# Last layer as seven block products: 2048x1024 rows times a 1024x1024 four-bit weight, on one core

## The chip, the cores and the metric

The kernel runs on 1 core of one Trainium2 chip. The metric is device time in microseconds (us) of one execution; the median of several executions counts. Times of single instructions come from one profiled execution.

## The reference

Two layers, each added to its input. The change is in the second one; the first is shown by its end only.

```python
x = x + xattn(layernorm(x), ctx, ctx, pos, mask, Wq, Wk, Wv, Wo)      # ends in 2048x4096 @ 4096x1024
x = x + ffn(layernorm(x), qweight, qzeros, scales, bias)

def ffn(x, qweight, qzeros, scales, bias):                           # x: 2048 x 1024
    w = (qweight[:, None, :] >> shifts & 15).reshape(1024, 1024)     # 4-bit numbers out of int32 words
    W = repeat(scales, 128) * (w - repeat(zeros, 128))
    return x @ W + bias
```

All is float32. The kernel makes each float32 product of a high and a low part per operand (hi*hi + hi*lo + lo*hi), so one 128x128 by 128x512 block costs three matmuls.

## The kernel before

The end of the kernel has two stages. The **output projection** (attention times Wo, added onto the rows of x) is already done as seven block products instead of eight, in the order M1, M7, M4, M5, M3, M2, M6. Each has 16 steps (PAIRS), so there are 112 steps (STEPS), numbered s = 0 to 111. One step is `block_step`: 8 blocks of rows, each into its own bank of `ps` (PSUM), three matmuls of 512 columns each (lines 823 to 825), 24 matmuls in all. The row tiles 0 to 7 are called EVEN, 8 to 15 ODD; their sums grow in `rows`.

Every engine walks the same steps in an order written out by hand, and each step passes through all of them. SP loads the left operand into `xring` (`load_left`) and the right one into `wraw` (`load_right`), two buffers each, and waits ahead of each for the low part two steps back. ACT (`step_hi`, lines 1045 and 1050) waits until TensorE has finished step s - 2, and writes the high parts into `a_parts` and `b_parts`, two slots each. VectorE (`step_lo`, line 1365) subtracts for the left low part, GpSimd (`step_lo`, line 1664) for the right one; in M1, M7, M4, M3 and M6 GpSimd first adds two right blocks (`right_summed`, line 1676). TensorE waits for both low parts. After each product VectorE adds the eight banks onto `rows` (`product_out`, line 1483), in the step with s % 16 == 1; products that go to two places are first copied by ACT into `spare` (line 1129) and added again later (line 1490). M6's eight banks end in ODD rows, right half, after the last step.

Beside these steps the kernel before prepares the **last layer**: VectorE and ACT unpack W into `w_parts` (high and low part, `DENSE_AT`, lines 1495 to 1504), and the statistics of the layer norm of the EVEN rows are taken in steps 82 to 92 (`row_stats`, `inverse_std`). The last layer then goes row tile by row tile, r = 0 to 15: VectorE normalizes (`y_normalize`, line 1510, which reads every eighth word of a row), TensorE transposes eight 128x128 blocks (`y_fill`, line 847), ACT and VectorE split the result into high and low part, and TensorE multiplies with all of W: `dense(r)`, 2 halves x 8 blocks of k x 3 matmuls (`products`, lines 244 to 246). VectorE adds the result onto the row tile (line 1569), to which GpSimd has added the bias (line 1720), and SP stores it. Statistics of the ODD rows are taken during the first row tiles.

In the program, waits are semaphores: `eng.wait_ge(name, n)` stops that engine's whole queue until n is reached, and `.then_inc(name, n)` counts up when the instruction is done.

Of the kernel before, what the change touches and what calls it, by code (L numbers as in the profile page):

```python
# [15 lines left out]
P = 128  # L16
# [36 lines left out]
V_H0_N0, K_H0, V_H0_N1, V_H1_N1, K_H1, V_H1_N0 = 0, 8, 24, 32, 40, 56  # L53

# [14 lines left out]
def build(nc, x, ctx_t, x_tiles, x_pieces, pos, mask, wq, wk, wv, wo, qweight, qzeros, scales, bias, table, ident, out):  # L69
# [4 lines left out]
    with ExitStack() as stack:  # L74
# [44 lines left out]
        with ExitStack() as late:  # L119
# [5 lines left out]
            dense = sb_c("dense", [P, 4, E], F32)  # L125
            rows = sb_c("rows", [P, 16, E], F32)
            w_parts = sb_c("w_parts", [P, KT, 2, E], F32R)
            zero_words = sb_c("zero_words", [P, E // NIB], I32)
            bias_rows = sb_c("bias_rows", [P, E], F32)
            spare = sb_c("spare", [P, 8, NW], F32)  # L130

# [6 lines left out]
        sq_dram = dram("sq_scratch", [4, P, 4, S])  # L138

# [39 lines left out]
        packed, scale_rows = dense[:, 0, :].bitcast(I32), dense[:, 1, :]  # L179
        zeros_f, w_full = dense[:, 2, :].bitcast(I32), dense[:, 3, :]  # L180
        xn = [dense[:, i, :] for i in range(4)]
        x2t = [a_parts[:, i, :, :].rearrange("p l (k t) -> p l k t", k=KT) for i in range(2)]
# [47 lines left out]
        z_step, dq_step, wf_full, wf_hi, wf_lo = sem("z_step"), sem("dq_step"), sem("wf_full"), sem("wf_hi"), sem("wf_lo")  # L230
        y_norm, y_done, y_hi, y_lo = sem("y_norm"), sem("y_done"), sem("y_hi"), sem("y_lo")
# [4 lines left out]
        ffn_done, ffn_added, biased = sem("ffn_done"), sem("ffn_added"), sem("biased")  # L236
# [57 lines left out]
        DENSE_AT = (25, 28, 34, 37, 40, 43, 54, 57)  # L294


        @block.sync
        def _(sp):
# [281 lines left out]
            for s in range(4, STEPS):  # L580
# [17 lines left out]
                if s == 22:  # L598
                    sp.dma_start(zero_words[:, :],
# [5 lines left out]
            for r in range(16):  # L605
                if r < 15:
                    sp.wait_ge(ffn_added, 2 * r + 2)
                    sp.dma_start(o_rows[row_tile(r)], rows[:, r, :]).then_inc(out_stored, 16)
                else:
                    for n in range(2):  # L610
                        sp.wait_ge(ffn_added, 2 * r + n + 1)
                        sp.dma_start(o_rows[row_tile(r)][:, n * NW:(n + 1) * NW], rows[:, r, n * NW:(n + 1) * NW]
                                     ).then_inc(out_stored, 16)
            sp.wait_ge(out_stored, 17 * 16)
# [3 lines left out]
        def _(pe):  # L618
# [218 lines left out]

            def y_fill(f):
                r = f // 2
                pe.wait_ge(y_norm, r + 1)  # L840
                if f < 2:
                    pe.wait_ge(m_out, 48 + f + 1)
                else:
# [912 lines left out]
```

## Time and profile before

| | us |
|---|---|
| median of 3 runs | 2243.64 (2242.38 to 2246.56) |
| the profiled execution | 2245.39 |
| span of its first to last instruction | 2243.6 |
| TensorE busy | 2225.5 (99%) |
| VectorE, ACT, GpSimd busy | 1370.2, 1052.7, 1394.0 |
| output projection ends, last layer begins | at 2050.6 of the span |
| mean granted clock of TensorE | 0.998 of full speed |

The page of the profile gives busy time per engine and the costliest groups of instructions. Beside it the trace answers questions: instructions in order of time, groups by line, the chain of waits that ended last, and busy time, clock and DMA rate in chosen stretches. A matmul's printed duration is longer than the distance to the next one, since matmuls are pipelined: what a step costs is read from the distance of its repeats.

### The profile page before, as it was taken

Reading aid. Unit: us, or ns where it says so; the run is one execution under the profiler, and the core shown is the slowest. Engines: PE = TensorE matmul, PEld = TensorE weight load, DVE = VectorE, ACT = ScalarE, POOL = GpSimd, SP = SyncE. Lnnn points to the kernel's source line nnn. Section 1 sums busy time; section 2 is a strip of 40 time slices with the busy share of each in tenths; the row PEclk is TensorE's granted clock in tenths of the full one; section 3 lists DMA queues with packets and bytes.
Section 4 is the critical chain, followed back from the end, with each engine's and each line's share of the span. In section 5 each row is a group of like instructions: output and inputs, shape, how many; then the busy total and the mean of one; then the engine's idle time right before and its main releaser. Section 6 shows DMA issues by size and latency. Waiting matters only on the chain.

```text
span 2243.6 us, 33219 instructions
## 1 busy us (share of the span) xinstructions
PE 2225.5 (99%) x10582; PEld 1868.4 (83%) x10582; DVE 1370.2 (61%) x2537; ACT 1052.7 (47%) x2298; POOL 1394.0 (62%) x982
## 2 busy tenths in 40 slices
PE   9999999999999999999999999899999999999999
PEld 7888888888888888788888888788888888888887
DVE  4772575777777778877777777423675445453532
ACT  3222133766766667666666766522333323331100
POOL 2320553788888889888888888665663354454210
PEclk9999999999999999999999999999999999999999
DMA  7766675687888789888888888697554554452111
GB/s 269 257 234 221 238 268 193 211 252 241 243 261 238 242 247 276 251 260 243 242 243 252 244 239 253 189 321 263 198 186 152 163 195 151 159 192 69 47 47 47
DMA packets 300187, 476.71 MB, mean 212 GB/s; under 512 B 23600, under 2 KB 195920, under 8 KB 300112
## 3 DMA queue, kind: packets, MB, share of 16 engines
q1 hardware_dynamic: 285744, 439.60, 62.4%
q10 hardware_dynamic: 13600, 34.08, 3.9%
q0 software_dynamic: 768, 2.10, 0.2%
q8 instruction: 39, 0.64, 0.1%
q14 instruction: 36, 0.29, 0.0%
HBM read 303.70 MB, written 171.98 MB: 212 GB/s over the span
## 4 chain that ended last, share of the span: by engine, by line
PE 91%; DVE 3%; POOL 3%; DMA 1%; ACT 1%; issue 1%; SPq 0%; DVEq 0%; ACTq 0%; POOLq 0%
PE ps L244 22%; PE ps L245 22%; PE ps L246 21%; PE ps L823 9%; PE ps L825 8%; PE ps L824 8%; PE ps L847 1%; POOL rope_tmp L1587 1%; DMA left_scratch<-s_buf 0%; POOL s_buf L1587 0%; DVE rope_tmp L1188 0%; DVE rope_tmp L1189 0%; DVE rope_tmp L1187 0%; ACT wq_t L891 0%; DMA wraw<-in_L_xattn_Wo 0%
## 5 line engine op out<-in xcount | busy, mean ns | idle before, releaser
L244 PE MATMUL ps<-act_t,wq_t 128*128 128x512 f32 x1280 | 500.2, 391 | 1.2 <-DVE act_t L1250 0.6
L245 PE MATMUL ps<-act_t,wq_t 128*128 128x512 f32 x1280 | 499.5, 390 | 0.0
L246 PE MATMUL ps<-act_t,wq_t 128*128 128x512 f32 x1280 | 498.0, 389 | 0.0
L1664 POOL TENSOR_TENSOR b_parts<-wraw,b_parts 128x512 fp32r<-128x512 f32 x112 | 200.3, 1788 | 267.0 <-ACT b_parts L1050 267.0
L823 PE MATMUL ps<-b_parts,a_parts 128*128 128x512 f32 x896 | 349.2, 390 | 0.6 <-DVE a_parts L1365 0.3
L824 PE MATMUL ps<-b_parts,a_parts 128*128 128x512 f32 x896 | 348.8, 389 | 0.0
L825 PE MATMUL ps<-b_parts,a_parts 128*128 128x512 f32 x896 | 348.6, 389 | 0.0
L1365 DVE TENSOR_TENSOR a_parts<-xring,a_parts 128x1024 fp32r<-128x1024 f32 x112 | 146.6, 1309 | 304.8 <-ACT a_parts L1045 304.8
L1646 POOL TENSOR_TENSOR q_t<-pt_raw,q_t 128x1024 fp32r<-128x1024 f32 x124 | 302.4, 2439 | 43.8 <-ACT q_t L1028 40.8
L1587 POOL TENSOR_TENSOR rope_tmp<-rope_tmp 128x512 f32<-128x512 f32 x144 | 193.3, 1342 | 182.7 <-DVE rope_tmp L1189 182.7
L1045 ACT ACTIVATE a_parts<-xring 128x1024 fp32r<-128x1024 f32 x112 | 118.7, 1060 | 393.3 <-PE ps L825 393.3
L246 PEld LDWEIGHTS ps<-act_t,wq_t 128*128 128x128 f32 x1280 | 240.4, 188 | 50.9
L244 PEld LDWEIGHTS ps<-act_t,wq_t 128*128 128x128 f32 x1280 | 240.8, 188 | 49.8 <-DVE act_t L1250 1.8
L245 PEld LDWEIGHTS ps<-act_t,wq_t 128*128 128x128 f32 x1280 | 240.8, 188 | 44.9
L1010 ACT ACTIVATE probs<-scores,neg_max 128x256 f32<-128x256 f32 x512 | 254.1, 497 | 3.6 <-DVE neg_max L1354 3.5
L1187 DVE TENSOR_TENSOR rope_tmp<-ps,rope 128x512 f32<-128x512 f32 x144 | 99.4, 690 | 218.7 <-PE ps L246 211.7
L1002 ACT ACTIVATE q_t<-rope_tmp 128x512 fp32r<-128x512 f32 x128 | 81.1, 634 | 321.8 <-POOL rope_tmp L1587 321.8
L1020 ACT ACTIVATE probs<-probs,inv_sum 128x256 f32<-128x256 f32 x512 | 216.8, 494 | 3.0 <-DVE inv_sum L1361 3.0
L1640 POOL TENSOR_TENSOR q_t<-rope_tmp,q_t 128x512 fp32r<-128x512 f32 x128 | 196.7, 1537 | 5.2 <-ACT q_t L1002 5.2
L823 PEld LDWEIGHTS ps<-b_parts,a_parts 128*128 128x128 f32 x896 | 168.4, 188 | 36.4 <-issue 0.9
L824 PEld LDWEIGHTS ps<-b_parts,a_parts 128*128 128x128 f32 x896 | 168.4, 188 | 35.0
L825 PEld LDWEIGHTS ps<-b_parts,a_parts 128*128 128x128 f32 x896 | 168.4, 188 | 34.8
(143 smaller groups left out, 4379.4 us busy)
## 6 DMA issues: line engine op xcount, KB each, us to landing
sq_scratch<-scores SPq DMA_DIRECT2D x124, 512.0 KB, 3.0
pt_raw<-sq_scratch SPq DMA_DIRECT2D x496, 128.0 KB, 4.0
xring<-left_scratch SPq DMA_DIRECT2D x112, 512.0 KB, 3.7
left_scratch<-s_buf SPq DMA_DIRECT2D x64, 640.0 KB, 5.3
wraw<-in_L_xattn_Wq SPq DMA_DIRECT2D x64, 512.0 KB, 4.6
wraw<-in_L_xattn_Wo SPq DMA_DIRECT2D x64, 512.0 KB, 4.5
v_scratch<-kv_t ACTq DMA_DIRECT2D x32, 512.0 KB, 3.4
k_scratch<-kv_t ACTq DMA_DIRECT2D x32, 512.0 KB, 5.0
```

The source lines that it names most:

```text
L244: eng.matmul(dst, lh, rh, start=(k == first), stop=False)
L245: eng.matmul(dst, lh, rl, start=False, stop=False)
L246: mm = eng.matmul(dst, ll, rh, start=False, stop=(k == last))
L823: pe.matmul(dst, lh, rh, start=(begins and not onto), stop=False, skip_group_check=True)
L824: pe.matmul(dst, lh, rl, start=False, stop=False, skip_group_check=True)
L825: mm = pe.matmul(dst, ll, rh, start=False, stop=ends, skip_group_check=True)
L1010: e = act.activation(probs[:, par, j, qt, :], score_v[:, par, j, qt * S:(qt + 1) * S], ACT.Exp, bias=neg_max[:, par, j, qt:qt + 1], scale= ...
L1020: e = act.activation(probs[:, par, j, qt, :], probs[:, par, j, qt, :], ACT.Copy, scale=inv_sum[:, par, j, qt:qt + 1])
L1587: pool.tensor_tensor(tmp[:, 0, :], tmp[:, 0, :], tmp[:, 1, :], ALU.add).then_inc(done, 1)
L1640: pool.tensor_tensor(q_parts[:, c, j, 1, :], rope_tmp[:, 0, :], q_parts[:, c, j, 0, :].bitcast(F32), ALU.subtract).then_inc(q_lo, 1)
L1646: pool.tensor_tensor(lo, pt_raw[:, u8 % 2, :], hi.bitcast(F32), ALU.subtract).then_inc(pt_lo, 1)
L1664: pool.tensor_tensor(b_parts[:, s % 2, 1, :], wraw[s % 2][:, 0:NW], b_parts[:, s % 2, 0, :].bitcast(F32), ALU.subtract).then_inc(right_lo, 1)
```

## The change

The last layer is done as seven block products too, with 4 steps of k each (KS = 4), so 28 steps, s = 112 to 139, in the order D_M1, D_M2, D_M6, D_M7, D_M4, D_M5, D_M3. A step has again 8 banks and 24 matmuls of 512 columns. The left operands are sums and differences of blocks of y (the normalized rows, transposed), the right ones of W.

- **W.** VectorE unpacks W in steps 25 to 56; GpSimd forms the four sums of its blocks (`weight_sum`, one of 128x512 in each of the steps 28 to 31, 38 to 41, 46 to 49, 57 to 60); SP stores all seven right operands to DRAM (`w_dram`, 12 transfers, 7.3 MB) in steps 33, 43, 51 and 62. In the last layer they are loaded back, 256 KB a step, into four half buffers of `wraw`.
- **First rows (EVEN).** Statistics in steps 82 to 88, normalized by ACT in steps 89 to 92 (`row_scaled`), two row tiles a step, transposed by VectorE (`turn_row`, 32x32 blocks; it reads words 8 apart and writes `turned`), stored to DRAM in 16 transfers of 256 KB (steps 93 to 100), and their first half loaded into `left_c` (steps 97 to 103). The bias is added by GpSimd (rows 0 to 5) and VectorE (6 and 7).
- **Second rows (ODD).** They are complete only after step 111. Statistics, normalization, 8 turns and 16 stores lie in steps 112 to 119; the first sum of them, which D_M6 needs at step 120, is `first_sum` on GpSimd in steps 118 to 121.
- **Low parts, sums, output.** ACT writes high parts (`dense_hi`, right operand first), VectorE the left low part (`dense_lo`) and the left sums (`dense_sum`, one 128x1024 operation ahead of each step of D_M6, D_M7, D_M5 and D_M3), GpSimd the right low part, and adds the product kept in `spare` twenty-four times (`add_second`). VectorE takes out eight banks after each product (`dense_out`), at the second step of the next one.
- The 128 transposes on TensorE, their splitting on ACT and VectorE, and the splitting of all of W are gone.

The diff, cut to what the steps of the last layer are made of:

```diff
+        SUMS_AT = (28, 38, 46, 57)
+        STATS_AT = (82, 83, 84, 85, 86, 86, 87, 87)
+        EVEN_AT = (89, 89, 90, 90, 91, 91, 92, 92)
+        BIAS_AT = (90, 91, 92, 93, 94, 95)
```

SP in the steps of the projection:

```diff
+                if s - 5 in SUMS_AT:
+                    k = SUMS_AT.index(s - 5)
+                    sp.wait_ge(w_summed, 4 * k + 4)
+                    sp.dma_start(w_dram[k, :, 0:4, :], w_sums).then_inc(w_stored, 16)
...
+                if 93 <= s < 101:
+                    sp.wait_ge(y_turned, 8)
+                    j, a0 = (s - 93) // 2, (s - 93) % 2 * 2
+                    for a in (a0, a0 + 1):
+                        store_turned(sp, 0, 2 * j, 2 * j + 2, a, turned_stored[j])
```

SP in the last layer (`dense_left_in` of a D_M6 step waits until the four stores of its k have landed, `turned_stored[k]` >= 128, and then loads `main[k]` and `left_b[:, k]`):

```diff
+            for s in range(STEPS, END):
+                d, k = dense_part(s)
+                if s + 2 < END:
+                    dense_left_in(s + 2)
+                if s + 3 < END:
+                    dense_right(s + 3)
+                if s == STEPS + KS + 1:
+                    sp.wait_ge(y_turned, 16)
+                    for j in range(2):
+                        for a in range(2):
+                            store_turned(sp, 1, 2 * j, 2 * j + 2, a, turned_stored[j])
+                elif s in (STEPS + KS + 2, STEPS + KS + 3):
+                    j = s - STEPS - KS
+                    for a in range(4):
+                        store_turned(sp, 1, 2 * j, 2 * j + 2, a, turned_stored[j])
...
```

TensorE:

```diff
+            def dense_step(s):
+                d, k = dense_part(s)
+                pe.wait_ge(left_lo, s + 1)
+                pe.wait_ge(right_lo, s + 1)
...
+                        elif d == D_M2:
+                            pe.wait_ge(d_copied, i + 1)
+                        else:
+                            pe.wait_ge(d_out, 8 * (d - 2) + i + 1)
...
```

ACT in the last layer:

```diff
+            for s in range(STEPS, END):
+                dense_hi(s)
+                if s == STEPS + 1:
+                    root(3, 8, 4)
+                    act.wait_ge(y_turned, 8)
+                if s == STEPS + 2:
+                    for r in range(8, 11):
+                        row_scaled(xn[:, r % 4, :], r)
+                    root(4, 12, 4)
...
+                if s == STEPS + KS + 1:
+                    act.wait_ge(y_turned, 16)
+                    for j in range(2):
+                        for a in range(2, 4):
+                            store_turned(act, 1, 2 * j, 2 * j + 2, a, turned_stored[j])
+                if s == STEPS + KS:
+                    act.wait_ge(m_added, 32)
+                    for i in range(8):
+                        bank_ready(act, D_M1, i)
+                        act.activation(spare[:, i, :], ps[:, i, :], ACT.Copy).then_inc(d_copied, 1)
```

VectorE (`dense_sum` of a D_M6 step waits for `s1_made` >= k + 1; what is left out at STEPS + 2 does for rows 12 to 15 what stands above for rows 8 to 11):

```diff
+            def turn_row(src, r):
+                dve.transpose(turned_v[:, r % 8], src.rearrange("p (b i k) -> p k b i", b=4, k=KT)).then_inc(y_turned, 1)
...
+            for s in range(STEPS, END):
+                d, k = dense_part(s)
+                if k == 1:
+                    if d > D_M2:
+                        dense_out(d - 1)
+                dense_lo(s)
+                if s + 1 < END:
+                    dense_sum(s + 1)
+                if s == STEPS:
+                    product_out(M6)
+                    for r in range(8, 12):
+                        dve.wait_ge(m_out, 48 + r - 8 + 1)
+                        half_stats(r, 1)
+                elif s == STEPS + 1:
+                    inverse_std(2, 8, 4)
+                    mean_scaled(8, 4)
+                elif s == STEPS + 2:
...
+                if STEPS + 2 <= s < STEPS + 5:
+                    for r in ((8,), (9, 10, 11), (12, 13, 14, 15))[s - STEPS - 2]:
+                        dve.wait_ge(y_act, r + 1)
+                        turn_row(xn[:, r % 4, :] if r < 12 else left_b[:, r % 4, :], r)
+                elif s in (STEPS + 6, STEPS + 7):
+                    for r in (2 * (s - STEPS), 2 * (s - STEPS) + 1):
+                        row_biased(r)
```

GpSimd:

```diff
+            def first_sum(k):
+                pool.wait_ge(main_in[k], 2 * 16)
+                pool.wait_ge(side_in[k], 32)
+                pool.tensor_tensor(left_b[:, k, :], left_b[:, k, :], main[k], ALU.add).then_inc(s1_made, 1)
...
+            for s in range(STEPS, END):
+                d, k = dense_part(s)
+                step_lo(s)
+                if STEPS + 2 <= s < STEPS + 6:
+                    pool.wait_ge(y_act, 8 + s - STEPS - 1)
+                    add_bias(8 + s - STEPS - 2)
+                elif STEPS + 6 <= s < STEPS + 10:
+                    first_sum(s - STEPS - 6)
+                elif d == D_M7:
...
+                    for i in (2 * k, 2 * k + 1):
+                        add_second(i, rows[:, ODD + i, NW:E])
```

## Rows read from the trace of the kernel before

**Rows 1.** The page: busy time of each engine (part 1) and mean DMA rate (part 3).
```profile
PE 2225.5 (99%) x10582; PEld 1868.4 (83%) x10582; DVE 1370.2 (61%) x2537; ACT 1052.7 (47%) x2298; POOL 1394.0 (62%) x982
...
HBM read 303.70 MB, written 171.98 MB: 212 GB/s over the span
```
**Rows 2.** The chain that ended last: start us, us, engine, tile, line.
```profile
2050.61 0.45 PE ps L847 x4
...
2076.45 0.87 PE ps L847 x8
...
2240.15 0.24 PE ps L246
2240.42 0.69 DVE rows L1569
```
**Rows 3.** Timeline of VectorE, end of the projection: start us, us, [idle before].
```profile
2035.42 1.23 DVE L1365 TENSOR_TENSOR a_parts<-xring,a_parts 128x1024 fp32r<-128x1024 f32 x1 [4.21 <-ACT a_parts L1045]
2040.86 1.23 DVE L1365 TENSOR_TENSOR a_parts<-xring,a_parts 128x1024 fp32r<-128x1024 f32 x1 [4.21 <-ACT a_parts L1045]
2045.88 5.46 DVE L1483 TENSOR_TENSOR rows<-ps,rows 128x512 f32<-128x512 f32 x8 [3.80 <-PE ps L825]
...
2068.17 3.64 DVE L1213 BATCH_NORM_STATS2 stats<-rows 128x6 f32<-128x512 f32 x6
```
**Rows 4.** Timeline of ACT and GpSimd, same steps.
```profile
2039.76 1.06 ACT L1045 ACTIVATE a_parts<-xring 128x1024 fp32r<-128x1024 f32 x1 [3.86 <-PE ps L825]
2040.73 0.62 ACT L1050 ACTIVATE b_parts<-wraw 128x512 fp32r<-128x512 f32 x1
...
2037.75 1.29 POOL L1676 TENSOR_TENSOR wraw<-wraw 128x512 f32<-128x512 f32 x1
2041.42 1.81 POOL L1664 TENSOR_TENSOR b_parts<-wraw,b_parts 128x512 fp32r<-128x512 f32 x1 [2.38 <-ACT b_parts L1050]
2043.19 9.45 POOL L1720 TENSOR_TENSOR rows<-rows,bias_rows 128x1024 f32<-128x1024 f32 x4
```
**Rows 5.** Timeline of VectorE at step 92: the layer norm of eight row tiles.
```profile
1937.90 0.71 DVE L1221 BATCH_NORM_AGGREGATE mean_var<-stats 128x2 f32<-128x12 f32 x8
...
1940.29 0.17 DVE L1235 TENSOR_TENSOR inv_std<-ln_tmp 128x8 f32<-128x8 f32 x1
```
**Rows 6.** VectorE by line and form, whole span: its transposition.
```profile
L1371 DVE STREAM_TRANSPOSE scores<-probs 128x1024 f32<-128x1024 f32 x124 | 154.4, 1245 | 4.2 <-ACT probs L1020 0.3
```
**Rows 7.** Timeline: VectorE beside GpSimd, two pairs, and VectorE alone.
```profile
1589.17 1.81 POOL L1664 TENSOR_TENSOR b_parts<-wraw,b_parts 128x512 fp32r<-128x512 f32 x1 [2.01 <-ACT b_parts L1050]
1589.75 1.78 DVE L1495 TENSOR_SCALAR dense<-dense 128x1024 int32<-128x1024 int32 x1
...
1948.21 1.81 POOL L1664 TENSOR_TENSOR b_parts<-wraw,b_parts 128x512 fp32r<-128x512 f32 x1 [3.56 <-ACT b_parts L1050]
1948.79 2.25 DVE L1510 TENSOR_SCALAR dense<-rows,mean_var,inv_std 128x1024 f32<-128x1024 f32 x1
...
2066.99 1.26 DVE L1510 TENSOR_SCALAR dense<-rows,mean_var,inv_std 128x1024 f32<-128x1024 f32 x1
```
**Rows 8.** DMA by issue: tiles, count, KB each, median us to landing.
```profile
xring<-left_scratch SPq DMA_DIRECT2D x112, 512.0 KB, 3.7
wraw<-in_L_xattn_Wo SPq DMA_DIRECT2D x64, 512.0 KB, 4.5
...
out<-rows SPq DMA_DIRECT2D x2, 256.0 KB, 2.0
```
**Rows 9.** Stretches: busy us of each engine, granted clock, DMA share, GB/s.
```profile
1426.00:1428.00 2.00, 2.00 (x18) 1.86 (x17) 0.78 (x2) 0.62 (x2) 0.04 (x1) 1.00 1.01 344
...
1432.00:1434.00 2.00, 0.00 (x0) 0.00 (x0) 2.00 (x5) 1.84 (x6) 2.00 (x3) 1.00 0.00 0
1434.00:1436.00 2.00, 1.44 (x6) 1.20 (x7) 0.41 (x1) 0.98 (x3) 0.51 (x1) 0.89 0.23 81
1436.00:1438.00 2.00, 2.00 (x11) 1.80 (x9) 0.69 (x1) 0.00 (x0) 0.00 (x0) 0.50 1.02 242
```

More of the change, by code:

```diff
@@ L53 @@
 V_H0_N0, K_H0, V_H0_N1, V_H1_N1, K_H1, V_H1_N0 = 0, 8, 24, 32, 40, 56
+D_M1, D_M2, D_M6, D_M7, D_M4, D_M5, D_M3 = range(7)
+D_RIGHT = (4, 5, 1, 2, 3, 0, 6)
+KS = KT // 2
 TILES = ((0, 0), (1, 0), (0, 1), (1, 1))
@@ L604, in _ @@
                                  ).then_inc(bias_in, 16)
[L605 to L613, printed above, removed]
@@ L617, in _ @@
+            for i in range(8):
+                sp.wait_ge(d_out, 32 + i + 1)
+                store_half(8 + i, 1)
+            for i in range(8):
+                sp.wait_ge(d_out, 40 + i + 1)
+                store_half(i, 1)
+            sp.wait_ge(out_stored, 32 * 16)
         @block.tensor
@@ L1129, in product_copied, with root, row_scaled @@
                     act.activation(spare[:, i, :], ps[:, i, :], ACT.Copy).then_inc(m_spared, 1)
+            def root(value, first, n):
+                act.wait_ge(ln_var, value)
+                act.activation(ln_tmp[:, 1, first:first + n], ln_tmp[:, 0, first:first + n], ACT.Sqrt).then_inc(ln_root, 1)
+            def row_scaled(dst, r):
+                act.wait_ge(ln_less, max(r // 4, 1))
+                act.activation(dst, rows[:, r, :], ACT.Identity, bias=ln_tmp[:, 3, r:r + 1],
+                               scale=inv_std[:, r:r + 1]).then_inc(y_act, 1)
             for s in range(2, STEPS):
@@ L1153, in _ @@
-            for f in range(32):
-                dense_fill_hi(f)
-                if f == 11:
-                    act.wait_ge(ln_var, 3)
-                    act.activation(ln_tmp[:, 1, 8:16], ln_tmp[:, 0, 8:16], ACT.Sqrt).then_inc(ln_root, 1)
+                if s == 88:
+                    root(2, 0, 8)
+                if s in EVEN_AT:
+                    for r in range(8):
+                        if EVEN_AT[r] == s:
+                            if r >= 4:
+                                act.wait_ge(y_turned, r - 3)
+                            row_scaled(xn[:, r % 4, :], r)
@@ new lines, in dense_out @@
+            def dense_out(d):
+                for i in range(8):
+                    bank_ready(dve, d, i)
+                    if d == D_M6:
+                        dve.wait_ge(d_copied, i + 1)
+                        dst = spare[:, i, :]
+                    elif d == D_M2:
+                        if i < 6:
+                            dve.wait_ge(biased, i + 1)
+                        else:
+                            dve.wait_ge(biased_v, i - 5)
+                        dst = rows[:, EVEN + i, 0:NW]
+                    elif d == D_M3:
+                        dve.wait_ge(u_added, 16 + i + 1)
+                        dst = rows[:, EVEN + i, NW:E]
+                    elif d == D_M4:
+                        dve.wait_ge(u_added, 8 + i + 1)
+                        dst = rows[:, ODD + i, 0:NW]
+                    else:
+                        dve.wait_ge(u_added, i + 1)
+                        dst = rows[:, ODD + i, NW:E]
+                    dve.tensor_tensor(dst, ps[:, i, :], dst, ALU.add).then_inc(d_out, 1)
@@ L1577, in _ @@
+            dense_out(D_M3)
         @block.gpsimd
```

347 lines of the change are left out of this document (230 added, 117 removed).

## The prediction

> **What bounds the kernel now.** First the busy times: TensorE is busy for 99% of the span [rows 1], so the time is TensorE's work plus its waits. Then the chain that ended last: from 2050.61 to 2240.39 (2240.15 + 0.24) it is TensorE, with 0.87 us of transpositions in each row tile, and behind it one addition of 0.69 and a store [rows 2]. So the last layer is 189.8 us of TensorE and a tail of 3.2. Third, the timelines of one step of the projection: VectorE's low part returns after 2040.86 - 2035.42 = 5.44 us [rows 3], which is the price of 24 matmuls, 0.227 each. In every step VectorE waits 4.21 ahead of its low part, ACT 3.86, GpSimd 2.38 [rows 3, 4]: that is the cover for new work. The last step begins at 2050.61 - 5.44 = 2045.17; VectorE has its low part at 2042.09 and GpSimd at 2043.23, so they may be 3.1 and 1.9 late before TensorE waits.
>
> **The change part by part.** Below, 0 is the end of step 111 (2050.61); numbers are us.
>
> TensorE. 28 steps of 5.44 are 152.3 instead of 189.8: **-37.5**, if nothing is late. The tail stays: the last product's banks end 0.68 apart, VectorE adds each in 0.69 [rows 2, 3], and a store of 256 KB takes 2.0 [rows 8], as now.
>
> W. A sum on GpSimd takes 1.29 (the row of the same shape) and falls into its gap of 2.38 [rows 4]; sixteen of them would be 20.6 without that gap. Each of the four store groups is 1.84 MB, 5.3 at 344 GB/s [rows 9], in SP's queue ahead of loads that are issued two steps early and now land after 3.7 to 4.5 [rows 8]. Without that cover steps 33 and 43, which load 512 KB of right operand, lose some 2 each, so 0 to 4; I take 0.
>
> One turn. VectorE's transposition of 128x1024 takes 1.245 [rows 6], but that one reads 32 words side by side. The new one reads words 8 apart, as line 1510 does now. How much that costs is in [rows 7]: in both pairs VectorE begins while GpSimd is at work, waits, and goes on when GpSimd ends. Line 1495 (1024 words side by side) ends 1591.53 - 1590.98 = 0.55 after GpSimd; line 1510 (1024 words, 8 apart) 1951.04 - 1950.02 = 1.02 after it: 1.85 times. So a turn lies between 1.25 (line 1510 is slow for another reason) and 1.245 x 1.85 = 2.3; it handles as many words as the old one, which excludes less. I take **2.3**, since line 1510 reads these very rows in this very pattern. The Trainium skill (Advanced Engine Details and Errata, Memory Cachelines) says that SBUF is read in lines of 16 bytes and that a pattern which goes to another line with each access pays a penalty; words 8 apart are 32 bytes apart. By that rule the sum is the one of the forecast below, without it that of the first rival; [rows 7] agree with it, no row shows a transposition that reads so.
>
> First rows, steps 89 to 103. Two turns and a low part are 5.8 per step, more than 5.44, and VectorE's subtraction waits for GpSimd's bias addition of 2.37 (9.45 / 4) [rows 4] which begins in the meantime: in steps 91, 92 and 93 the low part comes about 6.5 after the step before has begun, three waits of 1.05. The eighth turn ends 4.5 after the start of step 92. SP waits for it with the loads of step 94 queued behind, and two stores go ahead of these; they are issued some 3.5 late and land behind 512 KB, which costs 1.9 more. Together **+5.0**; with turns of 1.25 (3.7 per step) nothing. DMA at steps 96 to 103 is 1.6 to 2.1 MB a step, 4.6 to 6.1 at 344 GB/s, inside the two steps that loads run ahead.
>
> Second rows, the head of the layer. VectorE's queue after step 111 decides. It holds: low part of 112, M6's eight additions (5.5, to 3.3), four half statistics (0.61 each, to 5.7), low part of 113 (to 6.95). Step 113 was due at 5.44: wait 1.6. Then the layer norm of four tiles (for eight it took 2.6, 1937.90 to 1940.46 [rows 5]), in which ACT stands at the root with the high parts of 114 queued behind; low part of 114 at 11.0, in time. Four more statistics and the second layer norm, to 15.8; turn of row 8, to 18.1; low part of 115 behind a bias addition on GpSimd, 19.8, due 17.95: wait 2.0. Three turns, low part of 116 at 27.9, due 25.35: wait 2.6. Four turns, to 37.1, low part of 117 at 38.3, due 33.45: wait 5.0. Sum **+11.2**. With turns of 1.25 the last turn ends at 29.65 and the waits are 1.6, 2.0, 0 and 0.75: +4.4.
>
> The way through DRAM. At 37.1 SP and ACT, both waiting for the last turn (ACT with the high parts of 118 behind it, still in time), issue eight stores of 256 KB, 2.1 MB, 6.1 at 344 GB/s. SP then waits for the first half, with the right operands of 121 and later queued behind, and issues loads of 1.05 MB, which queue behind the second half: they land at about 50. GpSimd's first sum (2.4, to 52.4) has the right low part of step 119 queued behind it: step 119 starts at 53.8, due 49.3: wait 4.5. Each further k moves 1.05 MB of stores, 1.05 of loads and 0.26 of right operand, 6.9; the second sum ends at 59.3, then VectorE's left sum, and behind that the eight additions of D_M2, of which TensorE needs the first for step 120: wait about 4. Step 121 loses about 1, step 122 none. Sum **+9.5**. These 9.2 MB need 27 at 344 GB/s and 38 at 242, the lowest rate of a full stretch [rows 9]: 0 to 11 more.
>
> D_M7 to D_M3. In steps 125, 133 and 137 VectorE has 5.5 of additions, a low part and a sum (1.23 each): 8.0 against 5.44 and a reserve of 3.1, less what GpSimd holds it up (up to 1.29): 0.1 to 1.4 each, **+2.5** with the fourth. In six steps GpSimd's three operations (3.9) and VectorE's two (2.2) exclude each other, 6.1 of 5.44: if all of that shows, 9 instead of 2.5.
>
> The clock. Between 1432 and 1434 TensorE did nothing; right after, the granted clock fell from 1.00 to 0.89 and 0.50 in the next stretches [rows 9], half of 2.4 GHz. Two such us lose one. The waits ahead of steps 115 to 121 are as long, but most slowed steps end before the next operand is there. I take **+1.5**, 0 to 5.
>
> Sum: -37.5 + 5.0 + 11.2 + 9.5 + 2.5 + 1.5 = **-7.8**. The profiled execution would go from 2245.39 to 2237.6 (span 2243.6 to 2235.8); the median of the runs shown lies 1.75 lower than that execution, so I predict 2243.64 - 7.8 = 2236.
>
> **The rivals.**
> - Cheap turns (1.25): -37.5 + 0 + 4.4 + 9 + 2.5 + 1.5 = -20: **2223.5**. For it: the only row of a transposition [rows 6]. Against: [rows 7].
> - Cheap turns, and the stores and loads land before they are missed: -37.5 + 4.4 + 2.5 = -30.6: **2213**. Against it: two transfers in a row, 2.0 and 3.7 at the least [rows 8], under 4 MB of others.
> - The DMA is slower, and the time ends **above before**: strips of 32 partitions in pieces of 1 KB move at the mean rate of the span, 212 GB/s [rows 1], so the 9.2 MB ahead of step 122 need 43 instead of 27: +16, **2252**, all of it in waits ahead of 119 to 122. It decides from 233 GB/s down (+12.3, 2248.1). For it: 242 in a full stretch. Against: 344 in another [rows 9].
> - VectorE and GpSimd hold each other up in D_M7 to D_M5: +6.5, **2242.5**, no change that shows. For it: 6.1 of 5.44. Against: the operations of both have reserves of a few us.
>
> **How the numbers follow.** A measurement of this kernel can tell about 0.2%, 4.5 us, from no change: faster is below 2239.1, slower above 2248.1. Chances: forecast 0.46 (own range 2229 to 2243: 0.36 faster, 0.08 same, 0.02 slower), cheap turns 0.27, all hidden 0.05, slow DMA 0.14 (0.12 slower, 0.02 same), mutual holding 0.08 (0.06 same, 0.02 faster). Together faster 0.70, same 0.16, slower 0.14. The range goes from cheap turns with a third less waiting (2216) to the DMA bound of 242 GB/s on the forecast and a little more (2249); it leaves out all hidden and most of slow DMA, 0.17.
>
> **What would show it.** The transposition's row in the last layer: 2.3 or 1.25. TensorE idle ahead of steps 91 to 94, with VectorE's low part as what ended it. In the last layer, idle of TensorE ahead of 113, 115, 116 and 117 ended by VectorE's low part, ahead of 119 by GpSimd's, and GpSimd's first sum waiting for a DMA. From step 122 on 5.44 a step. TensorE's work is wrong if a step takes longer than 5.44 without a wait. The prediction is wrong if waits stand in steps 28 to 62, if the loads of the ODD rows land much later than 13 after the last turn, or if the last product's stores end later than 3.2 after the last matmul.

## The result and the profile after

| | before | after |
|---|---|---|
| median of the runs side by side, us | 2245.10 | 2234.15 (2231.84 to 2235.26) |
| ratio, 95% interval | | 0.995 (0.9938 to 0.9962) |
| the profiled execution, us | 2245.39 | 2235.26 |
| its span, us | 2243.6 | 2233.5 |
| step 112 starts (last layer begins) | 2050.61 | 2052.52 |
| last matmul ends | 2240.39 | 2230.1 |
| last layer on TensorE | 189.8 | 177.6 |

The forecast was 2236, faster. The interval of the ratio lies below 1: the kernel is 0.4 to 0.6% faster. In the page of the changed kernel (busy time per engine), which answers [rows 1], TensorE is busy for 28.6 us less:

```profile
PE 2196.9 (98%) x10358; PEld 1838.8 (82%) x10358; DVE 1436.9 (64%) x2575; ACT 1094.6 (49%) x2339; POOL 1493.0 (67%) x1048
```

The last layer is 12.2 us shorter. Its 28 steps are 152.3 without waits, so 25.3 are lost in it; the forecast had 24.7 there (11.2 + 9.5 + 2.5 + 1.5). TensorE's own timeline shows where it stands (start us, us, in brackets the idle time before and what ended it):

```profile
2058.72 0.50 PE L976 MATMUL ps<-b_parts,a_parts 128*128 128x512 f32 x1 [0.60 <-DVE a_parts L1718]
...
2074.26 0.79 PE L976 MATMUL ps<-b_parts,a_parts 128*128 128x512 f32 x1 [4.36 <-DVE a_parts L1718]
2074.85 0.63 PE L977 MATMUL ps<-b_parts,a_parts 128*128 128x512 f32 x1
2075.28 0.63 PE L978 MATMUL ps<-b_parts,a_parts 128*128 128x512 f32 x1
...
2090.55 0.68 PE L976 MATMUL ps<-b_parts,a_parts 128*128 128x512 f32 x1 [2.24 <-DVE a_parts L1718]
...
2106.17 0.47 PE L976 MATMUL ps<-b_parts,a_parts 128*128 128x512 f32 x1 [2.85 <-POOL b_parts L1881]
...
2115.66 0.77 PE L976 MATMUL ps<-b_parts,a_parts 128*128 128x512 f32 x1 [3.77 <-DVE rows L1757]
```

These are the starts of steps 113, 115, 117, 119 and 120. The next matmul follows 0.43 after the one before (2074.85, 2075.28) instead of 0.227: behind this wait of 4.36 TensorE runs at about half its rate for 15 matmuls. But the chain of work that ended last, which answers [rows 2], doesn't go through these waits. It leaves TensorE ahead of step 112 and comes back at step 120 (start us, us, engine, tile, line):

```profile
2050.38 4.79 DVE rows L1634 x8
2055.16 2.38 DVE stats L1672 x4
...
2071.07 2.03 DVE turned L1662
...
2074.20 5.94 DVE turned L1662 x3
...
2081.25 8.15 DVE turned L1662 x4
2089.42 0.36 ACTq L345
2089.81 5.55 DMA y_scratch<-turned
...
2095.75 6.55 DMA left_b<-y_scratch
2102.44 2.38 POOL left_b L1960
2104.83 2.27 DVE left_m L1725
2107.10 2.27 DVE rows L1666 x2
2109.37 2.33 DVE a_parts L1718
2112.64 2.28 DVE left_m L1725
2114.91 0.61 DVE rows L1757
2115.66 0.77 PE ps L976
```

VectorE works from 2050.38 to 2089.4 with no more than two pauses of 0.27 (for ACT's roots), then come 13.0 us of DRAM (the last turn's end to the landing of the first loads), 2.4 of GpSimd, 10.7 of VectorE. So TensorE's idle times and its slow matmuls up to 2115.66 lie beside this path, and the question for the experiments is what the path consists of. Below, times in the last layer are counted from the start of step 112 of the same profile, since that start lay anywhere from 2049.8 to 2055.7 in the kernels below, most of which have the same work ahead of it. In the changed kernel the last turn ends at 36.9, step 120 starts at 63.1, step 121 at 71.4. The ratio behind a measured time is to the kernel before, run beside it (its medians were 2243.99 to 2244.60). The runs of one kernel lie 2 to 6 us apart, so a difference of a few us is read from the length of the last layer in the profile too; a table at the end of this section has both.

### The profile page after: what moved, and what is told of

The parts are those of the page before. It is cut to its first block, busy times and chain, and to the rows that moved or that the text cites. A ratio compares the mean times of both kernels' runs of the same rounds, so it can differ in the third digit from the quotient of the medians.

```text
span 2233.5 us, 33060 instructions
## 1 busy us (share of the span) xinstructions
PE 2196.9 (98%) x10358; PEld 1838.8 (82%) x10358; DVE 1436.9 (64%) x2575; ACT 1094.6 (49%) x2339; POOL 1493.0 (67%) x1048
## 4 chain that ended last, share of the span: by engine, by line
PE 83%; DVE 8%; POOL 4%; issue 2%; DMA 2%; ACT 1%; SPq 0%; ACTq 0%; DVEq 0%; POOLq 0%
PE ps L264 18%; PE ps L265 18%; PE ps L266 18%; PE ps L945 8%; PE ps L947 8%; PE ps L946 8%; PE ps L976 1%; PE ps L978 1%; PE ps L977 1%; POOL s_buf L1803 1%; DVE turned L1662 1%; DVE rope_tmp L1340 1%; ACT wq_t L1007 1%; POOL rope_tmp L1803 1%; DVE rope_tmp L1339 1%
## 5 line engine op out<-in xcount | busy, mean ns | idle before, releaser
L1881 POOL TENSOR_TENSOR b_parts<-wraw,b_parts 128x512 fp32r<-128x512 f32 x140 | 241.1, 1722 | 283.9 <-ACT b_parts L1166 227.6
L946 PEld LDWEIGHTS ps<-b_parts,a_parts 128*128 128x128 f32 x896 | 168.2, 188 | 34.8
```

The source lines that it names most:

```text
L946: pe.matmul(dst, lh, rl, start=False, stop=False, skip_group_check=True)
L1881: pool.tensor_tensor(b_parts[:, s % 2, 1, :], src, b_parts[:, s % 2, 0, :].bitcast(F32), ALU.subtract).then_inc(right_lo, 1)
```

## The experiments

Theory A: every wait in steps 113 to 120 is time of its own, as the forecast added them up. Theory B: one path counts, VectorE's queue, DRAM, GpSimd's sum. Four kernels were made to tell them apart.

**High parts first.** Steps 113 to 138, but the first of a product, begin with the eight products that need no low part.

```diff
-                pe.wait_ge(left_lo, s + 1)
-                pe.wait_ge(right_lo, s + 1)
...
+                order = [(i, j) for j in range(3) for i in range(8)]    # j: hi*hi, hi*lo, lo*hi
+                pe.wait_ge(left_hi, s + 1)
+                pe.wait_ge(right_hi, s + 1)
...
```

> In steps 113 to 138 that are not the first of a product TensorE makes the eight products of high by high part first, which need no low part (1.8 us of work), then the rest; the output is the same. Theory A (sum): the waits of 113, 115, 117 and 119 shrink by up to 1.8 each (0.6 + 1.8 + 1.8 + 1.8 = 6.0) and the slow matmuls with them: 2224 to 2228. Theory B (one path): the last turn ends within 0.5 of where it did, step 120 starts at the same time after the end of the projection, and only 0 to 2 is won behind it (waits of 0.35 and 0.94): 2232 to 2234.

Measured 2234.02, ratio 0.9961 (0.9947 to 0.9975). The wait of 113 was gone, that of 115 3.47 instead of 4.36, but new ones of 1.82 and 1.09 for ACT stood at steps 116 and 118; the last turn ended at 36.9 and step 120 started at 63.3. Theory A falls: relieving TensorE ahead of step 120 is worth nothing. (The layer became 2.0 shorter, all of it behind step 120.)

**Turns that read side by side.**

```diff
-                act.activation(dst, rows[:, r, :], ACT.Identity, ...
+                act.activation(dst.rearrange("p (k b i) -> p k b i", b=4, k=KT),
+                               rows[:, r, :].rearrange("p (b i k) -> p k b i", b=4, k=KT), ACT.Identity, ...
...
-                dve.transpose(turned_v[:, r % 8], src.rearrange("p (b i k) -> p k b i", b=4, k=KT))
+                dve.transpose(turned_v[:, r % 8], src.rearrange("p (k b i) -> p k b i", b=4, k=KT))
```

> ACT writes the normalized row already in the order in which the turn wants it (it reads words 8 apart, writes side by side), so that the turn reads 32 words side by side; the output is the same. If the distance of the words makes a turn 2.1 us, its row falls to about 1.25; if the form of the operation makes it, the row stays at 2.1 and the time at 2234. Theory A (sum: each wait of TensorE in steps 113 to 120 is time of its own): the wait of step 115 shrinks by 0.9, that of step 117 (2.24) and its 8 slow matmuls (1.6) go, those of 119 and 120 stay: 2229.5. Theory B (one path: VectorE's queue from 2050.3 to the last turn at 2089.4 without a gap, then 13 us through DRAM, then GpSimd's sum up to step 120; TensorE's earlier waits lie inside it): the last turn ends 8 x 0.87 = 7.0 earlier and step 120 starts 6 to 7 earlier: 2228. Both: the wait of 0.77 at step 94 goes. ACT's row, now 1.17, may grow, which costs up to 2.

Measured 2233.35, 0.9952 (0.9935 to 0.9968). The distance of the words makes the turn's price. The first line is VectorE by line and form in the changed kernel (count, busy us, mean ns of one), the second the same row of this one:

```profile
L1662 DVE STREAM_TRANSPOSE turned<-xn 128x1024 f32<-128x1024 f32 x12 | 25.1, 2135 | 0.6 <-ACT xn L1249 0.4
```

```profile
L1663 DVE STREAM_TRANSPOSE turned<-xn 128x1024 f32<-128x1024 f32 x12 | 14.7, 1237 | 9.8 <-ACT xn L1249 9.8
```

2.1 against 1.24 us, and 1.24 is the old transposition of [rows 6]. The rule that the forecast weighed (the Trainium skill, Advanced Engine Details and Errata, Memory Cachelines) agrees; it gives no size. But the price only moved. ACT's timeline in this kernel, three rows scaled in step 114:

```profile
2064.96 6.88 ACT L1249 ACTIVATE xn<-rows,ln_tmp,inv_std 128x1024 f32<-128x1024 f32 x3 [1.08 <-DVE ln_tmp L1660]
```

That is 2.29 each instead of the 1.17 of the changed kernel there. The second root stood behind it, TensorE waited 6.12 at step 115, and the first rows lost 2.1 more than in the changed kernel (idle of 3.99 instead of 1.86). The last turn ended at 33.0 and step 120 started at 60.1, so turns that were 7.0 cheaper bought 3.0 there and 4.2 in the whole layer, and the first rows took 2.1 of that back. The median, 0.8 lower, is no clear gain.

**The bias of the ODD rows on GpSimd, later.**

```diff
-                if STEPS + 2 <= s < STEPS + 6:
-                    pool.wait_ge(y_act, 8 + s - STEPS - 1)
-                    add_bias(8 + s - STEPS - 2)
...
+                for r in {6: (8, 9), 10: (10,), 11: (11,)}.get(s - STEPS, ()):
+                    pool.wait_ge(y_act, r + 1)
+                    add_bias(r)
...
```

> GpSimd's four bias additions of ODD rows 8 to 11 go from steps 114 to 117 to steps 118 (two), 122 and 123; the output is the same. In the changed kernel two operations of 128x4 words on VectorE took 1.29 and 2.29 us instead of 0.16 in step 114, each beside such an addition. Expected in both theories: these rows fall to 0.16 to 0.2. Theory A (sum): the wait of step 115 falls from 4.36 to about 1.1 and its 14 slow matmuls (2.9) go: 2228. Theory B (one path): the last turn ends 3.2 to 4.4 earlier, and so does step 120: 2230 to 2231; where the wait of 115 was, the waits of 119 and 120 keep what they had or grow.

It was made for these lines of VectorE and GpSimd in step 114 of the changed kernel:

```profile
2066.82 0.16 DVE L1382 TENSOR_TENSOR ln_tmp<-ln_tmp 128x4 f32<-128x4 f32 x1
2067.02 1.29 DVE L1384 TENSOR_SCALAR ln_tmp<-ln_tmp 128x4 f32<-128x4 f32 x1
2068.34 2.29 DVE L1386 TENSOR_TENSOR inv_std<-ln_tmp 128x4 f32<-128x4 f32 x1
...
2066.98 1.30 POOL L1881 TENSOR_TENSOR b_parts<-wraw,b_parts 128x512 fp32r<-128x512 f32 x1 [1.23 <-ACT b_parts L1271]
2068.23 2.39 POOL L1939 TENSOR_TENSOR rows<-rows,bias_rows 128x1024 f32<-128x1024 f32 x1
```

Operations of four words per partition end when GpSimd's operation that began just before them ends (2068.31 and 2068.28, 2070.63 and 2070.62). Measured 2233.97, 0.9961 (0.9947 to 0.9975). Line 1386 fell to 0.16, the wait of 115 to 2.28, and the last turn ended at 35.0, 1.9 earlier. Step 120 still started at 63.2: the two additions in step 118 (6.72) now held VectorE's additions there, which took 6.76 instead of 2.35. Of line 1384 nothing went, since a low part on GpSimd holds it.

**No way through DRAM.** The stores of the turned rows are left out, and the loads read other data.

```diff
-                    sp.wait_ge(turned_stored[k], 8 * 16)
-                    dense_main(s, 1, 2 * k, s - 3)
+                    sp.wait_ge(y_turned, 13 + k)
+                    dense_main(s, 0, 2 * k, s - 3)
...
```

> Leaves out the sixteen stores of the turned ODD rows; the loads of D_M6, D_M7 and D_M4 read the EVEN rows' data instead, so the ODD half of the operands is not the reference's. The loads wait only until VectorE has turned the row that lies in their target. This takes the way through DRAM off the path. Forecast of the recorded prediction for this way: 9.5. Both theories: the waits of 119 (2.85) and 120 (3.77) and some 3 us of slow matmuls behind them go: 2224 to 2227; what is left are the waits of 113 to 117 and their slow matmuls, 7.2 + 4.5. If instead VectorE's and GpSimd's own work in steps 118 to 121 makes these waits, less than 4 is won: over 2230.

Measured 2237.48, 0.9973 (0.9962 to 0.9984): not faster, and both theories fall. Steps 118 and 119 began without a wait, and then TensorE waited 7.39 for step 120, which started at 62.5. VectorE and GpSimd in that stretch:

```profile
2099.08 3.41 DVE L1711 TENSOR_TENSOR left_m<-left_b,left_c 128x1024 f32<-128x1024 f32 x1
2102.42 5.66 DVE L1652 TENSOR_TENSOR rows<-rows,bias_rows 128x1024 f32<-128x1024 f32 x2
2108.00 2.28 DVE L1704 TENSOR_TENSOR a_parts<-left_m,a_parts 128x1024 fp32r<-128x1024 f32 x1
2110.20 3.36 DVE L1711 TENSOR_TENSOR left_m<-left_b,left_c 128x1024 f32<-128x1024 f32 x1
...
2098.03 3.38 POOL L1946 TENSOR_TENSOR left_b<-left_b,left_m 128x1024 f32<-128x1024 f32 x1
...
2103.61 3.39 POOL L1946 TENSOR_TENSOR left_b<-left_b,xring 128x1024 f32<-128x1024 f32 x1
...
2109.16 3.31 POOL L1946 TENSOR_TENSOR left_b<-left_b,xring 128x1024 f32<-128x1024 f32 x1
```

Five of VectorE's operations of 1.2 take 14.7 us here: the sums and low parts on GpSimd stand beside them, and D_M2's banks, which step 120 needs, come behind. Theory C was formed from this: **two paths of nearly the same length end ahead of step 120**, DRAM with GpSimd's sum, and VectorE's queue of steps 118 to 121 (turns go into both); shortening one shows the other. (Why its median lies 3 above the changed kernel stays open; its profiled execution was the fastest of eight, 2233.79, and its layer 0.8 shorter.)

**The sums on VectorE, and both paths at once.** VectorE makes the first sum itself, and adds the bias of rows 12 to 15 in step 117:

```diff
                 if d == D_M6:
+                    dve.wait_ge(main_in[k], 2 * 16)
+                    dve.wait_ge(side_in[k], 32)
+                    dve.tensor_tensor(left_b[:, k, :], left_b[:, k, :], main[k], ALU.add).then_inc(s1_made, 1)
                     dve.wait_ge(s1_made, k + 1)
...
-                elif s in (STEPS + 6, STEPS + 7):
+                elif s == STEPS + 5:
```

> VectorE makes the first sums of D_M6 itself, right ahead of its left sums (GpSimd made them, 2.37 to 3.40 each), and adds the bias of rows 12 to 15 in step 117, where it is idle, instead of 118 and 119; the output is the same. In the first four runs step 120 started 60.1 to 63.3 after the start of step 112, without the way through DRAM as well (62.5), where VectorE took 11.1 us for four operations that take 4.8 alone, GpSimd's sums beside them. Theory C (two paths of nearly the same length end ahead of step 120: DRAM with GpSimd's sum, and VectorE's queue of steps 118 to 121, which GpSimd's sums hold up): both get shorter, the wait of step 119 goes, step 120 starts at 56 to 59, time 2228 to 2230. Rival (the DMA alone decides): the first loads land where they did, step 120 starts at 61 or later, time 2232 to 2234.

> The edit before together with the one that leaves out the sixteen stores of the turned ODD rows and loads the EVEN rows' data in their place, so that the ODD half of the operands is not the reference's. Theory C: each alone leaves the other path, together they take both: steps 118 to 120 start without a wait, step 120 starts at 43.5 + 8.1 (waits of 113 to 117) + 4.6 (their slow matmuls) = 56, time 2224 to 2227. If step 120 still starts at 62, something that neither edit touches makes it late, and the time stays at 2233.

Measured 2232.20, 0.9945 (0.9928 to 0.9962), and with both 2225.06, 0.9915 (0.9899 to 0.9932). Step 120 started at 60.7, and with both at 56.05, where 56 was expected. TensorE's line at its start, with the sums on VectorE, without the way through DRAM, and with both (step 112 began at 2052.03, 2051.76 and 2051.96):

```profile
2112.76 0.77 PE L976 MATMUL ps<-b_parts,a_parts 128*128 128x512 f32 x1 [4.44 <-DVE rows L1760]
```

```profile
2114.30 0.77 PE L967 MATMUL ps<-b_parts,a_parts 128*128 128x512 f32 x1 [7.39 <-DVE rows L1743]
```

```profile
2108.01 0.47 PE L967 MATMUL ps<-b_parts,a_parts 128*128 128x512 f32 x1 [0.84 <-DVE rows L1746]
```

The layer became 0.8 shorter with only the way through DRAM left out, 2.9 with only the sums on VectorE, and 9.8 with both; the second edit is worth 7.1 of time on top of the first. So theory C holds. The first run by itself missed: 60.7 lies between the theory and its rival, and 2232.20 in the rival's range, since VectorE then stood waiting for the second pair of loads with D_M2's banks queued behind.

**The bias beside the turns.** GpSimd's bias additions go to steps 115 and 116, on top of the run with the sums on VectorE.

```diff
...
+                if s in (STEPS + 3, STEPS + 4):
+                    for r in ((8, 9, 10), (11,))[s - STEPS - 3]:
+                        pool.wait_ge(y_act, r + 1)
+                        add_bias(r)
```

> The first edit of this group, and GpSimd's bias additions of rows 8 to 11 in steps 115 (three) and 116 (one), beside VectorE's turns, instead of 114 to 117; the output is the same. Theory C: in step 114 VectorE's operations of 128x4 words take 0.2 at most instead of 1.29 and 2.29, the last turn ends some 3 earlier, and since nothing else holds step 120 any more, this shows: 2 to 3 below the first of this group, 2225 to 2228. Rival: turns beside three bias additions get longer by as much as was won, time as the first of this group.

Measured 2236.62, 0.9961 (0.9947 to 0.9975): slower by 4.4 than the run with the sums on VectorE, on which it builds, and by 3.9 in the layer. Neither the theory nor its rival had this. GpSimd was done with its low part of step 115 and began the additions while VectorE was still in the layer norm. VectorE, and GpSimd's three additions:

```profile
2070.49 2.31 DVE L1386 TENSOR_TENSOR inv_std<-ln_tmp 128x4 f32<-128x4 f32 x1
2072.83 2.26 DVE L1656 TENSOR_TENSOR ln_tmp<-mean_var,inv_std 128x4 f32<-128x4 f32 x1
2075.12 2.27 DVE L1659 TENSOR_SCALAR ln_tmp<-ln_tmp 128x4 f32<-128x4 f32 x1
...
2070.37 7.00 POOL L1942 TENSOR_TENSOR rows<-rows,bias_rows 128x1024 f32<-128x1024 f32 x3
```

Three additions, three small operations of 2.3; the last turn ended at 40.9. The miss shows the holding better than a hit would have.

**ACT writes apart instead of reading apart.** On the changed kernel, with turns that read side by side.

```diff
+                act.activation(dst.rearrange("p (k b i) -> p b i k", b=4, k=KT),
+                               rows[:, r, :].rearrange("p (b i k) -> p b i k", b=4, k=KT), ACT.Identity, ...
```

> As the run in which turns read side by side, but ACT reads the row side by side and writes the words where the turn wants them (next words 512 bytes apart); the output is the same. Turns 1.24 as in that run. If it is only reading apart that costs, ACT's row stays at 1.17 (it was 2.29 there), the first rows lose no more than in the changed kernel, the last turn ends some 7 earlier, and theory C gives a step 120 at 58 to 60: time 2230. If writing apart costs ACT as much as reading apart, time 2233.

Measured 2230.59, 0.9936 (0.9920 to 0.9953). ACT by line and form, in the changed kernel and in this one:

```profile
L1249 ACT ACTIVATE xn<-rows,ln_tmp,inv_std 128x1024 f32<-128x1024 f32 x12 | 14.2, 1232 | 1.1 <-DVE ln_tmp L1659 1.1
```

```profile
L1249 ACT ACTIVATE xn<-rows,ln_tmp,inv_std 128x1024 f32<-128x1024 f32 x12 | 25.6, 2237 | 1.1 <-DVE ln_tmp L1660 1.1
```

Writing apart, 2.24, costs what reading apart does. The last turn ended at 31.9, step 120 started at 58.7. The time came out as forecast for the case without ACT's price; the mechanism expected for it did not.

**Banks early, bias after the layer norm; then without this bias.** On top of the run with the sums on VectorE; the second kernel leaves four additions out:

```diff
+                    pool.wait_ge(y_act, 13)
+                    add_bias(2 * (s - STEPS) + 2)
+                    add_bias(2 * (s - STEPS) + 3)
...
+                if s == STEPS + 7:
+                    dense_out(D_M2, (0, 1))
+                if s == STEPS + 8:
+                    dense_out(D_M2, (4, 5, 6, 7))     # and banks 2, 3 ahead of the sums of step 121
```

> On top of the run with the sums on VectorE: GpSimd's bias additions of rows 8 to 11 wait until ACT has scaled row 12, that is until VectorE's second layer norm is over, and stand in steps 115 and 116; VectorE takes out D_M2's first four banks before it stands waiting for the loads of step 121. The output is the same. Theory C: the operation of 128x4 words that took 2.3 takes 0.2, the last turn ends 2 earlier (34.8 after the start of step 112 instead of 36.9); step 120 no longer waits for banks, step 121 starts at 61 instead of 66; time 2226 to 2229. Rival: the loads of step 121 land no earlier, since the DMA is full: step 121 at 65, time 2231.

> As the run in which VectorE takes the banks of D_M2 out early, but the four bias additions of rows 8 to 11 on GpSimd are left out, so that these rows lack the bias. In that run the held operation of the layer norm was gone, but the low parts of steps 115 and 116 took 2.73 and 3.24 instead of 1.18, and the last turn ended 38.4 after the start of step 112 instead of the 34.8 that was expected. Theory (the additions hold whatever VectorE does beside them other than a turn, and moving them only moves the hold): both low parts fall to 1.2, the last turn ends at 34.8, step 120 starts at 59 instead of 62.6, time 2227. Rival (these low parts were late for another reason, such as the turns around them): they keep 2.7 and 3.2, the last turn stays at 38, time 2231.

Measured 2230.95, 0.9935 (0.9921 to 0.9948), and without these four additions 2227.37, 0.9924 (0.9911 to 0.9938). In the first, line 1386 took 0.17, but the last turn ended at 38.4 instead of 34.8 and step 121 started at 65.5. These are the rival's numbers (65 and 2231), but not for its reason, a full DMA, as the second kernel shows. (The 62.6 and 59 in its expectation are where step 120 went on behind a wait for its fifth bank; it began at 57.4 and 55.1.) VectorE's low parts of steps 115 and 116 in the first run, and in the second:

```profile
2074.10 2.73 DVE L1718 TENSOR_TENSOR a_parts<-left_c,a_parts 128x1024 fp32r<-128x1024 f32 x1
...
2082.90 3.24 DVE L1718 TENSOR_TENSOR a_parts<-left_m,a_parts 128x1024 fp32r<-128x1024 f32 x1
```

```profile
2072.64 1.18 DVE L1718 TENSOR_TENSOR a_parts<-left_c,a_parts 128x1024 fp32r<-128x1024 f32 x1
...
2079.82 1.20 DVE L1718 TENSOR_TENSOR a_parts<-left_m,a_parts 128x1024 fp32r<-128x1024 f32 x1
```

The last turn then ended at 34.8 and step 121 started at 62.5, where the theory had 61. Moving GpSimd's addition moves the holding. It is free beside VectorE's turns and beside its statistics: four of these took 2.46 with an addition of 2.42 beside them in step 114 of the changed kernel, and 2.46 without one two steps before.

**ODD rows apart, and one k first.** On top of the first of the two kernels above, bias additions included, ACT writes apart in the ODD rows alone, two rows ahead of the second root; then, on top of it, only the first k's four stores go ahead of the first loads.

```diff
+                if r >= 8:
+                    dst = dst.rearrange("p (k b i) -> p b i k", b=4, k=KT)
+                    src = src.rearrange("p (b i k) -> p b i k", b=4, k=KT)
```

```diff
-                    for j in range(2):
-                        for a in range(2):
-                            store_turned(sp, 1, 2 * j, 2 * j + 2, a, turned_stored[j])
+                    for a in range(2):
+                        store_turned(sp, 1, 0, 2, a, turned_stored[0])
```

> On top of the run before, in the ODD rows alone ACT writes the words where the turn wants them (2.2 a row instead of 1.2), so that eight turns read side by side (1.24 instead of 2.1), and ACT scales only two rows ahead of the second root. The output is the same. Theory C: the last turn ends up to 4 earlier, step 121 starts at 57 to 58, time 2222 to 2225. Rival: ACT, with 17.6 of scaling and 8.3 of high parts in steps 114 to 117, takes VectorE's place, and the last turn ends where it did: 2227 to 2228.

> On top of the run before, only the four stores of the first k go ahead of the first loads; those of each further k go one step later. The output is the same. If the way through DRAM is bound by the 2.1 MB stored ahead of the first loads, these land 2 to 3 earlier, and the time falls by as much. Theory C, in which step 121 with its own stores and loads decides: the first loads come earlier, those of the second k do not, time 0 to 2 above the run before.

Measured 2222.79, 0.9904 (0.9889 to 0.9919), the fastest kernel of this study, and 2229.40, 0.9939 (0.9925 to 0.9952). In the first the last turn ended at 31.9, and steps 117 to 124 began without a wait, step 121 at 59.5, where 57 to 58 was expected. The longest wait left in the head stands at step 116, behind 0.59 at 113 and 1.45 at 115:

```profile
2083.21 0.76 PE L976 MATMUL ps<-b_parts,a_parts 128*128 128x512 f32 x1 [4.84 <-ACT spare L1313]
```

It is for ACT, which copies D_M1's banks only after its last rows of 2.1: here ACT has taken VectorE's place, as the rival had it, though the time is the theory's. In the second, steps 122 and 123 waited for the third and fourth k (1.36 and 3.85). The first loads were not what counted. The loss, 6.6, was larger than the 0 to 2 expected: the later loads now came behind the later stores.

Both measures of every kernel, in us:

| kernel | median | last layer on TensorE |
|---|---|---|
| changed | 2234.15 | 177.6 |
| high parts first | 2234.02 | 175.6 |
| turns side by side | 2233.35 | 173.4 |
| bias later | 2233.97 | 176.4 |
| no DRAM | 2237.48 | 176.8 |
| sums on VectorE | 2232.20 | 174.7 |
| sums, no DRAM | 2225.06 | 167.8 |
| bias beside turns | 2236.62 | 178.6 |
| ACT writes apart | 2230.59 | 172.8 |
| banks early | 2230.95 | 172.5 |
| the same without this bias | 2227.37 | 169.4 |
| ODD rows apart | 2222.79 | 165.6 |
| one k first | 2229.40 | 172.0 |

## Why the prediction was right

**TensorE, -37.5.** Right: steps 121 to 124 of the changed kernel follow each other after 5.44.

**The turn, 2.3.** 2.1 was measured, and 1.24 with words side by side, 1.7 times where 1.85 was taken. The choice between the bounds was right. That the factor of another operation in [rows 7] carries over to a turn was a guess that held. Cheap turns would have needed another writer, and the experiments show what that costs on ACT.

**First rows, +5.0.** Mis-sized. TensorE's idle time in these steps was 0.77 (step 94) and 1.09 (step 96, where the profile names no releaser), against 0.33 at step 97 in the kernel before, so some +1.5. The first ended with GpSimd's low part, not VectorE's. The waits expected at 91 to 93 did not come:

```profile
1926.46 1.22 DVE L1516 TENSOR_TENSOR a_parts<-xring,a_parts 128x1024 fp32r<-128x1024 f32 x1
1927.76 4.25 DVE L1662 STREAM_TRANSPOSE turned<-xn 128x1024 f32<-128x1024 f32 x2
1931.94 1.17 DVE L1516 TENSOR_TENSOR a_parts<-xring,a_parts 128x1024 fp32r<-128x1024 f32 x1
```

VectorE's low parts come back after 5.48, the price of a step: two turns of 2.13 and a low part of 1.2 just fill it, and the low part began ahead of GpSimd's addition instead of behind it. With turns 0.2 cheaper than forecast and the low part not held, the three waits of 1.05 vanish. What remained is the wait at 94, 0.77 where 1.9 was expected.

**The head, +11.2, and DRAM, +9.5.** Right as a path, not as a list of waits. The forecast put the last turn at 37.1, the first loads at about 50, step 119 at 53.8; measured were 36.9, 49.9 and 53.65. Its step 121 (9 x 5.44 + 20.7) was 69.7, or 71.2 with its 1.5 for the clock; 71.4 was measured. But the single waits were 0.6, 4.36, 0 and 2.24 ahead of 113, 115, 116 and 117, where 1.6, 2.0, 2.6 and 5.0 were forecast. The cause is one that the sum did not hold, VectorE's small operations held up by 1.1 in step 113 and by 1.1 and 2.1 in step 114. The layer norm was sized from [rows 5], where GpSimd stood beside one small operation only. Most of it is made good by eight turns that were 0.2 to 0.3 cheaper, M6's additions of 4.9 instead of 5.5, and a low part of 115 of 1.2 instead of 1.7. That the last turn came within 0.2 of the forecast is in part luck. As the run with high parts first shows, such waits are shadows of VectorE's queue, and their sizes among each other decide nothing.

**W, 0.** 0.26 of idle at 1679.89: right.

**D_M7 to D_M3, +2.5.** From step 124 on 2.8 were lost. The profile names 1.3 of it as waits, 0.35 at step 125 and 0.95 at step 132; the rest is in gaps of 0.1 to 0.3 between matmuls, which it does not name. Of the places forecast (125, 133 and 137) only the first came: the size is right, the places are not.

**The clock, +1.5.** Mis-sized. Slow matmuls lost some 8 us in the last layer. The changed kernel in stretches (busy us of each engine, granted clock, DMA share, GB/s):

```profile
2076.00:2082.00 6.00, 6.00 (x18) 4.69 (x18) 6.00 (x5) 4.38 (x8) 1.71 (x1) 0.63 0.32 107
...
2112.00:2118.00 6.00, 2.34 (x6) 1.89 (x7) 6.00 (x8) 1.61 (x2) 3.55 (x2) 0.72 0.98 367
```

In the first stretch TensorE makes 18 matmuls where 26 fit at full clock. The 5.0 that slow matmuls lost ahead of step 120 lie beside the path and cost nothing. Step 120 itself, in the second stretch and behind it, took 8.2 instead of 5.44, and these 2.8 do count, where 1.5 was forecast; as the 1 expected at step 121 did not come, step 121 was 1.7 later than its 69.7.

**The rivals.** Cheap turns: excluded by the turn's row. Slow DMA, which decides from 233 GB/s down: excluded, 280 GB/s from 2094 to 2100 and 354 to 367 from 2100 to 2118 (the last stretch above). The mutual holding of VectorE and GpSimd was looked for in D_M7 to D_M5, where its price was small; it stood in step 114 and in 118 to 121, as the kernel without the way through DRAM showed. In sum, for the profiled execution: the last layer lost 25.3 where 24.7 was forecast, step 112 began 1.9 later than before where 5.0 was forecast, and the tail was 3.4 instead of 3.2, so it came 10.1 below the kernel before and not 7.8. Since the start of step 112 lies up to 5.9 apart in kernels with mostly the same work ahead of it, a miss of 2 is within what these profiles can tell.

## What to carry to other kernels

Where a stage begins with a chain over several engines, work out when its last link is done: the waits of the bounding engine along the way are its shadows, and relieving them wins nothing. When taking a path away changes nothing, take it away together with the next one before calling it free. A strided access or a held port is a price that moves with the work: move it to where an engine has nothing else to do, and look there for it.

## What the runs showed of the hardware

- A 128x1024 float32 operation that read words 32 bytes apart cost 2.1 instead of 1.24 on VectorE (a turn) and 2.3 instead of 1.2 on ACT. Writing words 512 bytes apart cost ACT 2.24.
- VectorE's small operations of step 114 waited for GpSimd's, down to 128x4 words (0.16 alone, 1.3 and 2.3 beside GpSimd), and so did its low parts; turns did not (three in 6.02 beside an addition of 2.39), nor statistics (2.46 for four), nor additions out of PSUM (eight in 4.86 beside a sum of 2.39). The Trainium skill (SBUF — State Buffer, SBUF: two separate sides) has an exclusive port pair, held for a whole instruction, against operations of VectorE with two inputs in SBUF or in a two-port mode: the rows agree, the turn has one input. Line 1384 has one input too and was held (1.29, where line 1375 of the same form and size took 0.17 alone); whether it ran in such a mode no run shows.
- Four stores of 256 KB took each queue 4.2 to 4.3 us to issue, where a load took 0.32 when little else moved and up to 1.76 behind other transfers. With one k first, the two stores ahead of the first loads took SP 0.82. In the changed kernel, SP and ACT behind the last turn:

```profile
2089.41 4.24 SPq L345 DMA_DIRECT2D y_scratch<-turned  x4
...
2089.42 4.31 ACTq L345 DMA_DIRECT2D y_scratch<-turned  x4
```
